# Attention with 16 x 8 heads on one core: steps of the fourth kind make four pairs of tiles in a row and the value product in one piece

## Chip, cores and metric

The kernel runs on one core of one Trainium2 chip. The metric is device time in microseconds (us); less is better. One execution was taken with the hardware profiler on; its rows are read below. TensorE is PE in the rows (its weight loads are PEld), VectorE is DVE, ScalarE is ACT, GpSimd is POOL and SyncE is SP.

## The reference, cut to what matters

```python
# x: [16 images, 128 channels, 32*32 pixels], fp32
hid = group_norm(x, 32 groups)
q, k, v = qkv_w @ hid + qkv_b            # 8 heads of 16 channels, 1024 pixels
weight = softmax((q * s).T @ (k * s))    # per image and head: 1024 x 1024
h = proj_w @ (v @ weight.T) + proj_b
x = x + h
# then, per image
x = x + conv_w @ gelu(rmsnorm(x)) + conv_b
x = x + ffn_w2 @ gelu(ffn_w1 @ rmsnorm(x) + ffn_b1) + ffn_b2
```

The change touches the attention alone: for each image and head a 1024 x 1024 table of scores, its maximum over the keys, its exponential, and the product with the values.

## The kernel before

**Units and steps.** A unit is one image with four of its heads; there are 32 units, two to an image (half 0 and half 1). A unit has 16 steps: two halves of 512 query pixels times eight chunks of 128 key pixels. In one step TensorE makes three sorts of products.

- Four score tiles S0 to S3 (`scores`, L714), one for each head: 128 keys by 512 queries, contraction over 64 rows. They go to PSUM banks 0, 1 and 2 in turn (`tile % BANKS`, `BANKS = 3`). ScalarE takes the exponential of each (L985) into `probs`. A score tile waits on `probs_ready` until the exponential of the tile three before it is done (L713), since that frees its bank.
- Four maximum tiles M0 to M3 (`maximum_scores`, L699): the same scores the other way round, 128 queries by 512 keys, made 13 steps ahead (`LEAD`), so that the maximum of each query is known before its scores are made. VectorE reduces each (L1093). They go round a ring of four PSUM banks (`RING_BANKS = (3, 4, 5, 7)`), and each waits on `max_taken` or another signal until whatever held the place four before it has been read (`wait_for_place`, L683).
- The value product V (`weigh_values`, L730): four matmuls, one for each head, each on 32 of the 128 columns of the array, which add the previous step's exponentials times the values to bank 6. Each is recorded as two, so a V of 512 columns has eight records. V waits for the last exponential of the previous step.

An S and an M use different halves of the array's rows when they stand side by side, and the trace shows them starting within 0.01 us of each other. The text calls these two a pair.

**Side jobs.** Small products that belong to other images (projections of queries, keys and values, the group statistics, the output projection) are put in the middle of a step (`side_jobs`, L628). A side job takes a place in the ring of four banks too, between M1 and M2 of its step (the loop at L306 counts it at `k == 2`). Steps of the fourth kind have a side job at two places only: step 3 and step 7 of half 0 of the images 0 to 13 (`GROUP_MEAN`, L639, and `GROUP_VAR`, L647), each a matmul of one column. Every step of the second kind has a side job in most of the kernel: not in the first unit and the first step of the second, and only in some steps of the last three.

**Order.** No scheduler is at work: each engine's instructions stand as they are written, and TensorE takes them in that order. There are four kinds of step, `s % 4` from 0 to 3:

```text
first  (s % 4 == 0):  S0 M0 M1 S1 S2 M2  job  V  S3 M3
second (s % 4 == 1):  M0 S0 S1 M1  job  M2 S2 S3 M3  V
third  (s % 4 == 2):  M0 S0 S1 M1 M2 S2  job  V  S3 M3
fourth (s % 4 == 3):  S0 M0 M1 S1  job  V[0:256]  M2 S2 S3 M3  V[256:512]
```

ScalarE takes the four exponentials of a step in the order of their tiles, and the copy of the finished sums (L927) and the side jobs' results stand between them. VectorE takes the four maxima of a step, and at some steps a few small operations (L1072, L1079, L1109, L1120). After the last unit a second part follows (L890 on): the rest of the block for all images.

The last unit makes maximum tiles no more from its step 3 on, since they run 13 steps ahead: there a step has only S and V.

Of the kernel before, what the change touches and what calls it, by code (L numbers as in the profile page):

```python
# [33 lines left out]
HALF = 512  # L34
# [14 lines left out]
HB = HIDDEN // 128  # L49
CONV, FIRST = 2, 4  # L50
EARLY_X = 3
QUARTER = 256


LAST_K, GROUP_MEAN, VALUES, GROUP_VAR, PROJ = (0, 1), (0, 3), ((0, 5), (0, 9)), (0, 7), ((0, 13), (1, 1))
# [58 lines left out]
def has_unit(u):  # L114
    return not is_number(u) or 0 <= u < UNITS
# [12 lines left out]
def build(nc, d):  # L128
    fp32, fp32r = mybir.dt.float32, mybir.dt.float32r
    ALU, ACT, AX = mybir.AluOpType, mybir.ActivationFunctionType, mybir.AxisListType  # L130
    with ExitStack() as ctx:
# [71 lines left out]
        def steps_of(part):  # L203

            return {None: range(STEPS), 0: range(5), 1: range(5, 7), 2: range(7, 10), 3: range(10, STEPS)}[part]
# [402 lines left out]
        def _(pe):  # L608
# [80 lines left out]
            def maximum_scores(u, s, k):  # L689
                unit, step = max_item(u, s)  # L690
                place = unit % RING
                if not has_unit(unit):
                    return
                j, key_half, p, chunk, tile = k % 2, k // 2, step % 2, step // 2, max_tile(u, s, k)
                used = slice(ROWS * j, ROWS * j + MAX_ROW)
                if step == 0 and k == 0:
                    pe.wait_ge(stack_in, unit * (16 * STACK_DMAS) + 16 * STACK_DMAS)
                wait_for_place(max_place[tile])
                nc.tensor.matmul(bank_of(max_place[tile]),  # L699
                                 q_stack[used, place, p, chunk % 4, chunk // 4, :],  # L700
                                 k_stack[used, place, p, HALF * key_half:HALF * key_half + HALF],
                                 start=True, stop=True).then_inc(max_ready, 1)

            def scores(u, place, s, k):

                if not has_unit(u):
                    return
                head, t, chunk, tile = score_head(k), s // NK, s % NK, u * TILES + 4 * s + k
                used = slice(ROWS * (head % 2), ROWS * (head % 2) + ROWS)
                p = head // 2  # L710
                if chunk == 0 and k == 0:
                    pe.wait_ge(rows_in, (NT * u + t + 1) * (16 * ROW_DMAS))
                at_least(pe, probs_ready, tile - BANKS + 1)  # L713
                nc.tensor.matmul(psum[:, tile % BANKS, :], k_stack[used, place, p, 128 * chunk:128 * chunk + 128],  # L714
                                 q_stack[used, place, p, :, t, :],
                                 start=True, stop=True).then_inc(scores_ready, 1)

            def weigh_values(u, parity, half, s, lo, hi):


                chunk = s % NK
                if lo == 0:
                    pe.wait_ge(probs_ready, u * TILES + (4 * s + 4))
                    if chunk == 0:
                        at_least(pe, acc_taken, u * NT + s // NK)
                    if s == 0 and half == 0:
                        pe.wait_ge(v_full, u + 2)
                for k in range(UNIT_HEADS):
                    g = score_head(k)
                    last = nc.tensor.matmul(acc[32 * g:32 * g + 32, lo:hi],  # L730
                                            values[:, parity, chunk, UNIT_HEADS * half + g, :],
                                            probs[:, (4 * s + k) % 8, lo:hi],
                                            start=(chunk == 0 and lo == 0), stop=(chunk == NK - 1),
                                            skip_group_check=True)
                if hi == HALF:
                    last.then_inc(pv_done, 1)

            def weigh_before(u, parity, half, s, lo, hi):

                if s == 0:  # L740
                    if has_unit(u - 1):
                        if half == 0:
                            weigh_values(u - 1, 1 - parity, 1, STEPS - 1, lo, hi)
                        else:
                            weigh_values(u - 1, parity, 0, STEPS - 1, lo, hi)
                elif has_unit(u):
                    weigh_values(u, parity, half, s - 1, lo, hi)

            def slot(b, parity, half, part=None):
                u = b * 2 + half  # L750
                for s in steps_of(part):
                    place = 2 * parity + half
                    if b == IMAGES - 1 and (half, s) == FIRST_CONV:
                        for k in range(3):
                            scores(u, place, s, k)
                        weigh_before(u, parity, half, s, 0, HALF)
                        pe.wait_ge(max_taken, UNITS * TILES)
                        pe.wait_ge(proj_taken, (IMAGES - 1) * NT)
                        pe.wait_ge(weights_split, 1)
                        convolve(0, 0)  # L760
                        convolve(0, 1)
                        scores(u, place, s, 3)
                        continue

                    if s % 4 == 0:
                        scores(u, place, s, 0)
                        maximum_scores(u, s, 0)
                        maximum_scores(u, s, 1)
                        scores(u, place, s, 1)
                        scores(u, place, s, 2)  # L770
                        maximum_scores(u, s, 2)
                        side_jobs(b, parity, half, s)
                        weigh_before(u, parity, half, s, 0, HALF)
                        scores(u, place, s, 3)
                        maximum_scores(u, s, 3)
                    if s % 4 == 1:
                        maximum_scores(u, s, 0)
                        scores(u, place, s, 0)
                        scores(u, place, s, 1)
                        maximum_scores(u, s, 1)  # L780
                        side_jobs(b, parity, half, s)
                        maximum_scores(u, s, 2)
                        scores(u, place, s, 2)
                        scores(u, place, s, 3)
                        maximum_scores(u, s, 3)
                        weigh_before(u, parity, half, s, 0, HALF)
                    if s % 4 == 2:
                        maximum_scores(u, s, 0)
                        scores(u, place, s, 0)
                        scores(u, place, s, 1)  # L790
                        maximum_scores(u, s, 1)
                        maximum_scores(u, s, 2)
                        scores(u, place, s, 2)
                        side_jobs(b, parity, half, s)
                        weigh_before(u, parity, half, s, 0, HALF)
                        scores(u, place, s, 3)
                        maximum_scores(u, s, 3)
                    if s % 4 == 3:
                        scores(u, place, s, 0)
                        maximum_scores(u, s, 0)  # L800
                        maximum_scores(u, s, 1)
                        scores(u, place, s, 1)
                        side_jobs(b, parity, half, s)
                        weigh_before(u, parity, half, s, 0, QUARTER)
                        maximum_scores(u, s, 2)
                        scores(u, place, s, 2)
                        scores(u, place, s, 3)
                        maximum_scores(u, s, 3)
                        weigh_before(u, parity, half, s, QUARTER, HALF)

            def product(out, weights, high, low):

# [5 lines left out]
            def convolve(c, t):  # L818

                if t == 0:  # L820
                    pe.wait_ge(act1_split, c + 1)
                at_least(pe, conv_taken, c * NT + (t - 1))
                half = slice(HALF * t, HALF * t + HALF)
                high, low = (act1_second_high, act1_second_low) if c == 1 else (act1_high, act1_low)
                product(psum[:, CONV_BANKS[t], :], (wconv_high[:, :], wconv_low[:, :]),
                        high[:, half], low[:, half]).then_inc(conv_ready, 1)
# [86 lines left out]
            nc.tensor.matmul(misc[:, 0:1], wp[:, :], params[:, V_B:V_B + 1], start=True, stop=True).then_inc(bias_ready, 1)  # L913
            pe.wait_ge(bias_taken, 1)
            run(pe, slot, lead_in, refine, project_last)


# [407 lines left out]
```

## Time and profile before

| | us |
|---|---|
| median of three runs | 1671.47 |
| lowest and highest | 1670.27, 1671.72 |
| the profiled execution, its own time | 1672.58 |
| its span, first to last instruction | 1670.6 |

| engine | busy us | share of the span |
|---|---|---|
| PE | 1606.7 | 96% |
| DVE | 1454.5 | 87% |
| ACT | 1341.3 | 80% |
| POOL | 335.6 | 20% |

The attention fills the span from 76.1 us (the first V) to 1419.7 us (the last V). A step takes some 2.6 us of it, four steps some 10.4 to 10.5 us. A timeline row gives the start, the duration and the engine; rows with "xN" merge N instructions that follow each other, and the duration then reaches from the first one's start to the last one's end. Durations of matmuls include the filling and draining of the array, so that the pace is read from one start to the next.

### The profile page before, as it was taken

How to read it: one execution, taken by the hardware profiler on the slowest of the kernel's cores; microseconds unless marked ns; L12 is line 12 of the kernel's file. 1: busy time of each engine (PE TensorE's matmuls, PEld its weight loads, DVE VectorE, ACT ScalarE, POOL GpSimd, SP SyncE). 2: the span in 40 equal slices, each digit the busy share in tenths (PEclk: the TensorE clock that was granted, in tenths of full speed). 3: DMA queues.
4: the chain of work that ended last, by engine and by line, in shares of the span. 5: the costliest groups of instructions: out<-in, count | busy, mean ns of one | idle time of the engine just before them, and what ended most of it. 6: DMA issues, size and time to landing. Idle time of an engine off the chain costs nothing.

```text
span 1670.6 us, 29685 instructions
## 1 busy us (share of the span) xinstructions
PE 1606.7 (96%) x10602; PEld 673.0 (40%) x10602; DVE 1454.5 (87%) x2415; ACT 1341.3 (80%) x2478; POOL 335.6 (20%) x411
## 2 busy tenths in 40 slices
PE   4999999999999999999999999999999998899999
PEld 2433333333333333333333333333333332455555
DVE  4999999999999999999999999999999994455552
ACT  2288888888888888888888888888888887666664
POOL 3101111111111111111121212121211122322220
PEclk9599999999999999999999999999999998999999
DMA  5233333333333333333333333333333320234332
GB/s 115 32 47 59 59 59 60 59 60 59 58 61 58 60 58 61 58 61 58 61 58 60 58 61 58 49 56 50 56 50 57 50 60 29 84 115 115 88 105 75
DMA packets 58610, 105.91 MB, mean 63 GB/s; under 512 B 32864, under 2 KB 33632, under 8 KB 58464
## 3 DMA queue, kind: packets, MB, share of 16 engines
q1 hardware_dynamic: 56160, 95.64, 33.8%
q10 hardware_dynamic: 2304, 8.39, 1.2%
q8 instruction: 84, 1.38, 0.4%
q14 instruction: 62, 0.51, 0.1%
HBM read 34.48 MB, written 9.05 MB: 26 GB/s over the span
## 4 chain that ended last, share of the span: by engine, by line
PE 89%; ACT 4%; DVE 3%; SPq 1%; issue 1%; DMA 1%; POOL 0%; DVEq 0%; ACTq 0%; POOLq 0%
PE psum L730 31%; PE psum L714 19%; PE psum L699 15%; PE psum L843 7%; PE psum L625 4%; ACT probs L985 4%; PE psum L814 2%; PE psum L816 2%; PE psum L815 2%; PE psum L617 2%; DVE maxes L1093 2%; PE psum L662 2%; PE psum L851 1%; SPq L357 1%; DMA q_stack<-rows 0%
## 5 line engine op out<-in xcount | busy, mean ns | idle before, releaser
L1093 DVE TENSOR_REDUCE maxes<-psum 128x1 f32<-128x512 f32 x2048 | 1270.7, 681 | 54.3 <-PE psum L699 45.9
L985 ACT ACTIVATE probs<-psum 128x512 f32<-128x512 f32 x2048 | 1093.2, 601 | 199.3 <-PE psum L714 180.3
L699 PE MATMUL psum<-k_stack,q_stack 62*128 62x512 f32 x2048 | 697.9, 442 | 1.7 <-DVE maxes L1093 0.9
L714 PE MATMUL psum<-q_stack,k_stack 64*128 64x512 f32 x2048 | 691.8, 439 | 5.3 <-ACT probs L985 4.2
L730 PE MATMUL psum<-probs,values 128*32 128x512 f32 (+1 forms) x5120 | 573.7, 520 | 22.0 <-ACT probs L985 22.0
L714 PEld LDWEIGHTS psum<-q_stack,k_stack 64*128 64x128 f32 x2048 | 326.8, 186 | 322.8 <-ACT probs L985 278.3
L699 PEld LDWEIGHTS psum<-k_stack,q_stack 62*128 62x128 f32 x2048 | 333.3, 188 | 250.9 <-DVE maxes L1093 188.2
L730 PEld LDWEIGHTS psum<-probs,values 128*32 128x32 f32 x5120 | 100.8, 108 | 225.1 <-issue 140.2
L479 POOL CAST parts<-neg_max 128x16 fp32r<-128x16 f32 x64 | 12.6, 197 | 554.9 <-DVE neg_max L1072 554.9
L843 PE MATMUL psum<-probs,first_weights 128*128 128x512 f32 x256 | 116.6, 598 | 0.9 <-DVE raw L1261 0.9
L995 ACT ACTIVATE probs<-psum,params_sb 128x512 f32<-128x512 f32 x128 | 82.3, 686 | 21.3 <-PE psum L816 14.9
L625 PE MATMUL psum<-hid,first_weights 128*128 128x512 f32 x128 | 75.8, 686 | 6.2 <-POOL hid L511 6.2
L528 POOL TENSOR_TENSOR x_sb<-attn,x_sb 128x512 f32<-128x512 f32 x32 | 41.2, 1290 | 177.9 <-ACT attn L970 177.5
L843 PEld LDWEIGHTS psum<-probs,first_weights 128*128 128x128 f32 x256 | 47.3, 189 | 60.8 <-issue 52.9
L814 PE MATMUL psum<-q_stack,q_high 128*128 128x512 f32 x128 | 57.5, 449 | 0.7 <-DVE q_stack L1194 0.7
L1200 DVE COPY sums<-psum 128x512 f32<-128x512 f32 x16 | 11.1, 692 | 52.0 <-PE psum L851 52.0
L1194 DVE TENSOR_TENSOR q_stack<-q_full,q_stack 128x1024 fp32r<-128x1024 f32 x16 | 19.6, 1226 | 36.8 <-ACT q_stack L1051 36.8
L1261 DVE SCALAR_TENSOR_TENSOR raw<-psum,params_sb,x_sb 128x512 f32<-128x512 f32 x32 | 24.0, 750 | 31.6 <-PE psum L843 31.6
L1030 ACT ACTIVATE hid<-x_sb 128x1024 f32<-128x1024 f32 x14 | 14.9, 1062 | 45.1 <-DVE x_sb L1164 45.1
L549 POOL TENSOR_TENSOR rms_out<-mean_eps,neg_halves 128x16 f32<-128x16 f32 x17 | 50.4, 2963 | 1.3
L816 PE MATMUL psum<-q_stack,q_low 128*128 128x512 f32 x128 | 50.4, 394 | 0.0
L815 PE MATMUL psum<-q_stack,q_high 128*128 128x512 f32 x128 | 50.3, 393 | 0.0
(95 smaller groups left out, 931.1 us busy)
## 6 DMA issues: line engine op xcount, KB each, us to landing
q_stack<-q_high SPq DMA_DIRECT2D x128, 128.0 KB, 4.0
k_stack<-k_high SPq DMA_DIRECT2D x128, 128.0 KB, 5.2
values<-inv_rms_rows SPq DMA_DIRECT2D x32, 512.0 KB, 5.1
x_sb<-in_x SPq DMA_DIRECT2D x16, 512.0 KB, 7.6
q_stack<-q_low SPq DMA_DIRECT2D x64, 128.0 KB, 6.3
k_stack<-k_low SPq DMA_DIRECT2D x64, 128.0 KB, 7.0
q_stack<-rows SPq DMA_DIRECT2D x512, 2.0 KB
attn<-raw SPq DMA_DIRECT2D x128, 64.0 KB, 2.3
```

Of the source, the lines that this page charges most:

```text
L549: nc.gpsimd.tensor_tensor(out=rms_out[:, :], in0=mean_eps[:, :], in1=neg_halves[:, :], op=ALU.pow).then_inc(rms_ready, 1)
L625: nc.tensor.matmul(qk_bank(c, n), weight[:, :], hid[:, HALF * t:HALF * t + HALF], start=True, stop=True).then_inc(qk_ready, 1)
L699: nc.tensor.matmul(bank_of(max_place[tile]), q_stack[used, place, p, chunk % 4, chunk // 4, :], k_stack[used, place, p, HALF * key_half:HA ...
L714: nc.tensor.matmul(psum[:, tile % BANKS, :], k_stack[used, place, p, 128 * chunk:128 * chunk + 128], q_stack[used, place, p, :, t, :], sta ...
L730: last = nc.tensor.matmul(acc[32 * g:32 * g + 32, lo:hi], values[:, parity, chunk, UNIT_HEADS * half + g, :], probs[:, (4 * s + k) % 8, lo ...
L814: nc.tensor.matmul(out, w_high, high, start=True, stop=False)
L815: nc.tensor.matmul(out, w_high, low, start=False, stop=False)
L816: return nc.tensor.matmul(out, w_low, high, start=False, stop=True)
L843: mm = nc.tensor.matmul(psum[:, OUT_BANK, :], w2[:, at:at + 128], act2(t, m), start=(m == 0), stop=(m == HB - 1))
L985: nc.scalar.activation(probs[:, tile % 8, :], psum[:, tile % BANKS, :], ACT.Exp, scale=SCALE).then_inc(probs_ready, 1)
L995: nc.scalar.activation(act2(t, m), psum[:, HIDDEN_BANKS[m], :], ACT.Gelu, bias=params[:, FFN_B1 + m:FFN_B1 + m + 1]).then_inc(act2_ready, 1)
L1093: nc.vector.tensor_reduce(maxes[:, chunk // 4, j, 4 * p + chunk % 4, key_half:key_half + 1], bank_of(max_place[max_tile(u, s, k)]), axis=A ...
```

## The change

In steps of the fourth kind the value product is no longer made in two pieces of 256 columns, one after S1 and one after M3. It is made in one piece of 512 columns behind M3, so that M2, S2, S3 and M3 follow directly on M0, S0, S1, M1 (and the side job, where there is one). The order is then that of the second kind, but for S0 and M0. Nothing else is changed; no other engine's instructions move.

```diff
 EARLY_X = 3
-QUARTER = 256
...
                         maximum_scores(u, s, 1)
                         scores(u, place, s, 1)
                         side_jobs(b, parity, half, s)
-                        weigh_before(u, parity, half, s, 0, QUARTER)
                         maximum_scores(u, s, 2)
                         scores(u, place, s, 2)
                         scores(u, place, s, 3)
                         maximum_scores(u, s, 3)
-                        weigh_before(u, parity, half, s, QUARTER, HALF)
+                        weigh_before(u, parity, half, s, 0, HALF)
```

Because `QUARTER` is gone, line numbers after it are one lower (L714 becomes L713, L730 becomes L729).

The order on PE shows it. First, a step of the fourth kind without a side job, from the last pair of the third kind to the first score tile of the next step, before:

```order
L714 MATMUL psum<-q_stack,k_stack 128x512 [waits probs_ready]
L699 MATMUL psum<-k_stack,q_stack 128x512 [waits max_taken]
L714 MATMUL psum<-q_stack,k_stack 128x512 [waits probs_ready]
L699 MATMUL psum<-k_stack,q_stack 128x512 [waits max_taken] x2
L714 MATMUL psum<-q_stack,k_stack 128x512 [waits probs_ready]
L730 MATMUL psum<-probs,values 32x256 [waits probs_ready]
L730 MATMUL psum<-probs,values 32x256 x3
L699 MATMUL psum<-k_stack,q_stack 128x512 [waits max_taken]
L714 MATMUL psum<-q_stack,k_stack 128x512 [waits probs_ready] x2
L699 MATMUL psum<-k_stack,q_stack 128x512 [waits max_taken]
L730 MATMUL psum<-probs,values 32x256 x4
L714 MATMUL psum<-q_stack,k_stack 128x512 [waits probs_ready]
```

The same place on PE in the changed kernel (L713 is S, L698 is M, L729 is V):

```order
L713 MATMUL psum<-q_stack,k_stack 128x512 [waits probs_ready]
L698 MATMUL psum<-k_stack,q_stack 128x512 [waits max_taken]
L713 MATMUL psum<-q_stack,k_stack 128x512 [waits probs_ready]
L698 MATMUL psum<-k_stack,q_stack 128x512 [waits max_taken] x2
L713 MATMUL psum<-q_stack,k_stack 128x512 [waits probs_ready]
L698 MATMUL psum<-k_stack,q_stack 128x512 [waits max_taken]
L713 MATMUL psum<-q_stack,k_stack 128x512 [waits probs_ready] x2
L698 MATMUL psum<-k_stack,q_stack 128x512 [waits max_taken]
L729 MATMUL psum<-probs,values 32x512 [waits probs_ready]
L729 MATMUL psum<-probs,values 32x512 x3
L713 MATMUL psum<-q_stack,k_stack 128x512 [waits probs_ready]
```

Eight matmuls of 256 columns have become four of 512, and five pairs now stand between one V and the next, where three and two stood. Second, on PE, step 7 of half 0 of an image, from M0 on, with its side job L647, before:

```order
L699 MATMUL psum<-k_stack,q_stack 128x512 [waits max_taken] x2
L714 MATMUL psum<-q_stack,k_stack 128x512 [waits probs_ready]
L647 MATMUL psum<-gn,first_weights 128x1 [waits max_taken,gn_mix]
L730 MATMUL psum<-probs,values 32x256 [waits probs_ready]
L730 MATMUL psum<-probs,values 32x256 x3
L699 MATMUL psum<-k_stack,q_stack 128x512 [waits max_taken]
L714 MATMUL psum<-q_stack,k_stack 128x512 [waits probs_ready] x2
L699 MATMUL psum<-k_stack,q_stack 128x512 [waits max_taken]
L730 MATMUL psum<-probs,values 32x256 x4
```

The same place on PE in the changed kernel, where the job's line is L646:

```order
L698 MATMUL psum<-k_stack,q_stack 128x512 [waits max_taken] x2
L713 MATMUL psum<-q_stack,k_stack 128x512 [waits probs_ready]
L646 MATMUL psum<-gn,first_weights 128x1 [waits max_taken,gn_mix]
L698 MATMUL psum<-k_stack,q_stack 128x512 [waits max_taken]
L713 MATMUL psum<-q_stack,k_stack 128x512 [waits probs_ready] x2
L698 MATMUL psum<-k_stack,q_stack 128x512 [waits max_taken]
L729 MATMUL psum<-probs,values 32x512 [waits probs_ready]
L729 MATMUL psum<-probs,values 32x512 x3
```

With a side job the two last maximum tiles now follow the job directly, with no V between them; the signals they wait for are the same as before.

## Rows read from the trace of the kernel before

**Rows 1.** The page, parts 1 and 2: busy us, and tenths in 40 slices.

```profile
PE 1606.7 (96%) x10602; PEld 673.0 (40%) x10602; DVE 1454.5 (87%) x2415; ACT 1341.3 (80%) x2478; POOL 335.6 (20%) x411
PE   4999999999999999999999999999999998899999
PEclk9599999999999999999999999999999998999999
```

**Rows 2.** Waits of PE over the span: us in total, times, longest us.

```profile
PE psum L730 <- ACT probs L985: 22.0, 100, 0.6
PE psum L714 <- ACT probs L985: 4.2, 9, 0.5
```

**Rows 3.** Timeline of PE, fourth kind, no job: start us, us, engine, line.

```profile
706.23 0.49 PE L714 MATMUL psum<-q_stack,k_stack 64*128 64x512 f32 x1
706.56 0.63 PE L714 MATMUL psum<-q_stack,k_stack 64*128 64x512 f32 x2
706.80 0.40 PE L699 MATMUL psum<-k_stack,q_stack 62*128 62x512 f32 x1
707.41 0.64 PE L730 MATMUL psum<-probs,values 128*32 128x256 f32 x8 [0.20 <-ACT probs L985]
707.98 0.50 PE L699 MATMUL psum<-k_stack,q_stack 62*128 62x512 f32 x1
...
708.64 0.64 PE L730 MATMUL psum<-probs,values 128*32 128x256 f32 x8
709.21 0.49 PE L714 MATMUL psum<-q_stack,k_stack 64*128 64x512 f32 x1
```

**Rows 4.** Timeline of ACT at the same place, from 706.5 to 707.7 us.

```profile
706.76 1.08 ACT L985 ACTIVATE probs<-psum 128x512 f32<-128x512 f32 x2 [0.38 <-PE psum L714]
```

**Rows 5.** Timeline of PE, second kind without a job, in unit 29.

```profile
1317.45 0.50 PE L714 MATMUL psum<-q_stack,k_stack 64*128 64x512 f32 x1
...
1318.64 0.99 PE L714 MATMUL psum<-q_stack,k_stack 64*128 64x512 f32 x2
1319.13 0.49 PE L699 MATMUL psum<-k_stack,q_stack 62*128 62x512 f32 x1
1319.56 1.07 PE L730 MATMUL psum<-probs,values 128*32 128x512 f32 x8
1320.56 0.50 PE L699 MATMUL psum<-k_stack,q_stack 62*128 62x512 f32 x1
```

**Rows 6.** Timeline of ACT there, from 1317.9 to 1318.9 us.

```profile
1317.99 1.09 ACT L985 ACTIVATE probs<-psum 128x512 f32<-128x512 f32 x2 [0.33 <-PE psum L714]
```

**Rows 7.** Timeline of PE, fourth kind with job L639, in unit 10.

```profile
496.73 0.50 PE L714 MATMUL psum<-q_stack,k_stack 64*128 64x512 f32 x1
...
497.63 0.38 PE L639 MATMUL psum<-mean_var,first_weights 128*128 128x1 f32 x2
497.94 0.64 PE L730 MATMUL psum<-probs,values 128*32 128x256 f32 x8
...
499.75 0.50 PE L714 MATMUL psum<-q_stack,k_stack 64*128 64x512 f32 x1
```

**Rows 8.** Timeline of DVE there: from 497.3 to 497.9 us, and to 498.5.

```profile
497.30 0.69 DVE L1093 TENSOR_REDUCE maxes<-psum 128x1 f32<-128x512 f32 x1 [0.17 <-PE psum L699]
497.30 1.29 DVE L1093 TENSOR_REDUCE maxes<-psum 128x1 f32<-128x512 f32 x2 [0.17 <-PE psum L699]
```

**Rows 9.** Timelines of DVE and PEld in the first maxima, one after the other.

```profile
48.51 0.68 DVE L1093 TENSOR_REDUCE maxes<-psum 128x1 f32<-128x512 f32 x1
49.23 0.28 PEld L699 LDWEIGHTS psum<-k_stack,q_stack 62*128 62x128 f32 x1 [0.32 <-DVE maxes L1093]
```

**Rows 10.** Timeline of PE in the last unit, without M: fourth kind, then second.

```profile
1374.54 0.50 PE L714 MATMUL psum<-q_stack,k_stack 64*128 64x512 f32 x1
1377.29 1.17 PE L714 MATMUL psum<-q_stack,k_stack 64*128 64x512 f32 x3
...
1411.07 0.73 PE L714 MATMUL psum<-q_stack,k_stack 64*128 64x512 f32 x3
1414.16 0.49 PE L714 MATMUL psum<-q_stack,k_stack 64*128 64x512 f32 x2
```

## The prediction, made before the changed kernel ran

> **What bounds the kernel now.** I read the page first. TensorE is busy for 96% of the span and at full tenths in nearly every slice of the attention, so what lengthens its line lengthens the kernel; VectorE comes next with 87%. The granted clock is at its upper level in nearly all slices [rows 1]. Then the waits of PE: it stood idle before V for 22.0 us, 100 times, always for an exponential, and before score tiles for 4.2 us in all [rows 2]. The 100 are steps of the fourth kind. There are 128 of these (four in each of 32 units); 28 have a side job (step 3 and step 7 of half 0, images 0 to 13), which fills the gap, and 100 have none: 96 in units 0 to 30 and all four of unit 31.
>
> Then the timeline of one such step, counted from S3 of the third kind at 706.23, the first tile behind a V. Two more pairs start at 706.56 and 706.80. The first piece of V starts only at 707.41, having waited 0.20 for the exponential of that S3; M2 and S2 follow 0.57 later at 707.98, the second piece at 708.64, and S0 of the next step at 709.21 [rows 3]. That is 2.98 us from V's end to V's end. No other wait of this size stands on PE between this step and the next fourth one, so a step of the fourth kind that grows by x makes the kernel grow by x.
>
> **What is removed.** Four matmuls a step, and one turn from tiles to V and back. From rows: a piece of 256 columns takes 0.57, the two 1.14, and one V of 512 columns 1.00 (1319.56 to 1320.56) [rows 3, 5]: 0.14 less. In the middle of a run, a pair follows a pair after 0.24 (706.56 to 706.80), but the first after V takes 0.33 and so does the last before V [rows 3]: runs of three and two pairs (0.90 + 0.66) become one run of five (0.33 + 3 x 0.24 + 0.33 = 1.38), 0.18 less. And the 0.20 of idle time ahead of V goes. That is 0.5 us a step, if PE could run freely.
>
> The Trainium skill has a rule for the second of these, on the page "TensorEngine Tiling (Array Packing)", Key Properties: changing the tiling mode, rather than just the tile, drains the engine. The trace agrees, with the 0.33 against 0.24. By the rule alone the change saves time; it is the mechanism of the second rival below.
>
> **What it runs into.** Score tiles have three banks. S2 waits for the exponential of the third kind's S3, and S3 for that of the S0 in its own step. Between them stood a piece of V, which took up just this time. Now PE reaches them early. The two exponentials end at 706.76 + 1.08 = 707.84 for the second [rows 4]; a waiting tile starts about 0.05 after (1317.99 + 1.09 = 1319.08, tile at 1319.13) [rows 5, 6]. So S3 and M3 start at 707.89 and not 708.32. V starts 0.43 behind a pair that had waited (1319.13 to 1319.56) and takes 1.00 [rows 5]: next S0 at 709.32, against 709.21. The step is 0.11 longer.
>
> The trace has this very order already, in steps of the second kind that have no side job. There five pairs stand in a row, and PE goes from S3 at 1317.45 to the first tile behind V at 1320.56 [rows 5]: 3.11 us against 2.98, 0.13 longer. ScalarE's times there are the same from the first tile on (0.54, then 1.09 for two exponentials, against 0.53 and 1.08) [rows 4, 6]. So the parts give 0.11 and the analogue 0.13, each with a rounding of 0.01; I take 0.115, nearer the parts, which are of this very step. **96 steps x 0.115 = 11.0 us.**
>
> The maximum tiles in these steps wait for nothing later: M3 takes the place of the third kind's M3, whose reduction ends 1.26 after the first tile (496.73 to 497.99) [rows 7, 8], while S3 starts at 1.66.
>
> **The 28 steps with a side job** are another matter. The job takes one of the four places of the ring, between M1 and M2. So M2 takes that of the third kind's M3, and M3 that of M0 in its own step. Before, V stood between and nobody waited. M0's reduction ends at 497.30 + 1.29 = 498.59 [rows 8]; a weight load that waits for VectorE starts 0.04 to 0.05 after it (48.51 + 0.68 = 49.19, then 49.23) [rows 9]. M3 therefore starts at 498.64, 0.24 later than S3 could. M2 is held as well, to 497.99 + 0.05 = 498.04, but S3 may not start before 498.40 anyway. V at 498.64 + 0.43 = 499.07, next S0 at 500.07, against 499.75 now [rows 7]: 0.32 longer. **28 x 0.32 = 9.0 us.** This is the least sure term, as no row shows M3 held so. If M0's reduction came in time the step would be 3.10 long against 3.02: 0.08, or 2.2 us for 28. I take 0.32, since VectorE reduces without a pause from M3 of the third kind on (1.29 for two, 0.60 each) and cannot come sooner.
>
> **The last unit** has no M from step 3 on. Its fourth step goes from 1374.54 to 1377.29, 2.75 us; a second-kind step with the new order, from 1411.07 to 1414.16, 3.09 [rows 10]. 0.34 longer, times four: **1.4 us**, between 0 (one of them hides behind the next part's first loads) and 1.8.
>
> **The sum:** 11.0 + 9.0 + 1.4 = 21.4 us. The profiled execution took 1672.58, which makes 1694.0; the median of three runs lies 1.1 lower: 1692.9.
>
> Nothing hides this. What is queued behind the waiting S3 on PE is M3, V and the whole next step. ScalarE gets S2 and S3 earlier than now, but it already idles before the next step's S0, so that buys nothing; VectorE needs 16 x 0.60 = 9.6 us of four steps' 10.4 [rows 8] and is not the end.
>
> **Rivals.**
>
> 1. *Slower, but by less:* M3 isn't held in the 28 steps. 11.0 + 2.2 + 1.4 = 14.6 us, 1686.1. Against it: the ring has four places, and the job takes one. 13%.
> 2. *Faster:* tiles flow at PE's pace. A fourth step would be 1.38 + 1.00 = 2.38 long: 0.60 less in 96 steps and 0.64 less in 28, together 75 us, so 1596; VectorE's 9.6 us for four steps wouldn't forbid it. This is what the rule on draining would give if nothing else bound. The point where it decides is the start of S3: 0.43 + 1.00 = 1.43 us stand behind it, so the step gets shorter only if S3 starts by 2.98 - 1.43 = 1.55 after the first tile. The rows put it at 1.66, since S0's bank is read only then. For the rival speaks only that the waits on PE now are short ones [rows 2]. 5%.
> 3. *No change:* a later wait gets shorter by as much as this one grows. All waits of V together were 22.0 us and go with the pieces; 4.2 us of the others is all that could give [rows 2], so 1692.9 would become 1688.7 at best, and it is within 0.2% only if M3's hold fell away and the analogue misled too. 2%.
> 4. *Much slower:* M3 is held in every fourth step, as in the 28: to 3.34 against 2.98, 0.36 x 96 = 34.6, with 9.0 and 1.4 45 us: 1716.5. It needs a reduction that ends 0.4 later than the rows say. 5%.
>
> The forecast has the remaining 75%.
>
> **How the numbers follow.** The predicted time is the forecast's, 1692.9. The low end takes in rival 1 without a good part of the last unit's term (1686.1 - 1.4 = 1684.7, rounded to 1684); the high end has 0.13 for 0.115 (1.4 us more), 1.8 for 1.4 in the last unit, and 0.37 for 0.32 in the 28 (1.4 us more): 1696.1, rounded to 1697. Beyond lie rivals 2, 3 and 4 with 12% between them. A measurement of this kernel can tell about 0.2%, 3.3 us, from no change. Slower by more: forecast, rivals 1 and 4, 93%. Within: 2%. Faster: 5%.
>
> **What would show it.** In the changed kernel's timeline, a fourth step without a job should look like the second kind's in unit 29: S2 about 1.18 and S3 about 1.66 after the first tile, V at 2.10, next tile at 3.10. With a job, M3 alone at 1.91, V at 2.34, next tile at 3.34. The waits of PE should name ScalarE at score tiles instead of V, and VectorE at M3 in 28 steps; four steps take 10.5 to 10.6 us for 10.4. PEclk should stay where it is, since the new idle times are 0.25 us long and the first unit, whose second-kind steps have such waits already, shows the upper level. The prediction is wrong if V starts within 1.98 us after the first tile, or if the steps with and without a job grow alike.

## The result: 13.6 us slower

| | median of runs, us | lowest and highest | profiled span, us |
|---|---|---|---|
| before | 1671.60 | 1670.27, 1672.01 | 1670.6 |
| changed | 1685.18 | 1684.14, 1685.42 | 1683.4 |

The ratio is 1.0081, its 95% interval 1.0064 to 1.0099, so the kernel is slower, as forecast, and by 13.6 us where the forecast had 21.4: the time lies inside the range, near its low end, at the time of the first rival (1686.1), though not for its reason. Some runs below had an execution in a slower state of the chip (one each of e3, e7 and c2): ratios and their intervals leave it out, the medians of those three would be 0.09 to 0.14 us lower without it, and the trace of e7_red_before is of such an execution and isn't read.

The page of the changed kernel, parts 1 and 2, answers to [rows 1]:

```profile
PE 1640.5 (97%) x9578; PEld 683.9 (41%) x9578; DVE 1465.3 (87%) x2415; ACT 1327.6 (79%) x2478; POOL 336.0 (20%) x411
PE   4999999999999999999999999999999998899999
PEclk9699999999999999999999999999999999999999
```

PE has 1024 records less and is *busy* 33.8 us more. That is the first thing to read here: busy time on PE is not work. A matmul's record lasts some 0.5 us while the next may start after 0.24 [rows 3], so PE can stand held for 0.2 us with no idle time on the page. The waits of the changed kernel show it (engine, line, what it waited for: us in total, times, longest), and answer to [rows 2]; the last row is of the weight loads:

```profile
PE psum L713 <- ACT probs L983: 4.7, 13, 0.5
PE psum L698 <- DVE maxes L1091: 0.9, 2, 0.5
...
PEld psum L713 <- ACT probs L983: 361.5, 582, 0.9
```

The 22.0 us ahead of V are gone, and PE's own waits for score tiles have hardly grown (4.2 to 4.7). It is the *weight loads* that tell of the new waits: those of score tiles waited 361.5 us for exponentials, where the kernel before has:

```profile
PEld psum L714 <- ACT probs L985: 278.3, 477, 0.9
```

A step of the fourth kind without a job, PE's timeline in the changed kernel, answers to [rows 3]:

```profile
522.77 0.50 PE L713 MATMUL psum<-q_stack,k_stack 64*128 64x512 f32 x1
522.78 0.73 PE L698 MATMUL psum<-k_stack,q_stack 62*128 62x512 f32 x2
523.11 0.62 PE L713 MATMUL psum<-q_stack,k_stack 64*128 64x512 f32 x2
523.35 0.61 PE L698 MATMUL psum<-k_stack,q_stack 62*128 62x512 f32 x2
523.96 0.99 PE L713 MATMUL psum<-q_stack,k_stack 64*128 64x512 f32 x2
524.45 0.50 PE L698 MATMUL psum<-k_stack,q_stack 62*128 62x512 f32 x1
524.88 1.06 PE L729 MATMUL psum<-probs,values 128*32 128x512 f32 x8
525.87 0.50 PE L713 MATMUL psum<-q_stack,k_stack 64*128 64x512 f32 x1
```

From the first tile S2 comes at 1.19, S3 (with M3) at 1.68, V at 2.11, the next step at 3.10. It was 2.98. And one with the job, in unit 10, step 3, the place of [rows 7]:

```profile
501.24 0.49 PE L713 MATMUL psum<-q_stack,k_stack 64*128 64x512 f32 x1
...
502.15 0.38 PE L638 MATMUL psum<-mean_var,first_weights 128*128 128x1 f32 x2
502.55 0.50 PE L698 MATMUL psum<-k_stack,q_stack 62*128 62x512 f32 x1
502.55 0.85 PE L713 MATMUL psum<-q_stack,k_stack 64*128 64x512 f32 x2
503.15 0.50 PE L698 MATMUL psum<-k_stack,q_stack 62*128 62x512 f32 x1
503.57 1.06 PE L729 MATMUL psum<-probs,values 128*32 128x512 f32 x8
504.57 0.50 PE L713 MATMUL psum<-q_stack,k_stack 64*128 64x512 f32 x1
```

M2 starts at 1.31, M3 alone at 1.91, V at 2.33, the next step at 3.33. VectorE's timeline there, the answer to [rows 8]:

```profile
501.80 1.29 DVE L1091 TENSOR_REDUCE maxes<-psum 128x1 f32<-128x512 f32 x2 [0.15 <-PE psum L698]
```

The second of these is the reduction of M0; it ends at 503.09, and M3 starts 0.06 later.

So both kinds of step have the shape that was forecast, to within 0.02 us. Where are the missing 8 us? From the start of each step's S0 to the next, in both traces, summed by sort of step (changed kernel less the kernel before; both traces are of one execution, so that their spans differ by 12.8 us and the medians by 13.6):

| | steps | forecast, us | measured, us |
|---|---|---|---|
| fourth kind without a job, units 0 to 30 | 96 | +11.0 | +10.2 |
| fourth kind with a job | 28 | +9.0 | +8.6 |
| all other steps of units 0 to 30 | 372 | 0 | -3.3 |
| last unit | 16 | +1.4 | -2.1 |
| before the first S0 | | 0 | -0.6 |
| after the last score tile | | 0 | -0.1 |
| span | | +21.4 | +12.8 |

### The profile page after: what moved, and what is told of

Read it like the earlier page. It is cut to its first block, busy times and chain, and to the rows that moved or that the text cites. A ratio compares the mean times of both kernels' runs of the same rounds, so it can differ in the third digit from the quotient of the medians.

```text
span 1683.4 us, 27637 instructions
## 1 busy us (share of the span) xinstructions
PE 1640.5 (97%) x9578; PEld 683.9 (41%) x9578; DVE 1465.3 (87%) x2415; ACT 1327.6 (79%) x2478; POOL 336.0 (20%) x411
## 4 chain that ended last, share of the span: by engine, by line
PE 95%; DVE 2%; ACT 1%; SPq 1%; issue 1%; POOL 0%; DMA 0%; ACTq 0%; DVEq 0%; POOLq 0%
PE psum L729 30%; PE psum L713 25%; PE psum L698 16%; PE psum L841 7%; PE psum L624 4%; PE psum L812 2%; PE psum L813 2%; PE psum L814 2%; PE psum L616 2%; PE psum L661 2%; DVE maxes L1091 1%; PE psum L849 1%; ACT probs L983 0%; PE psum L638 0%; PE psum L646 0%
## 5 line engine op out<-in xcount | busy, mean ns | idle before, releaser
L713 PE MATMUL psum<-q_stack,k_stack 64*128 64x512 f32 x2048 | 717.1, 443 | 5.4 <-ACT probs L983 4.7
L698 PE MATMUL psum<-k_stack,q_stack 62*128 62x512 f32 x2048 | 701.8, 442 | 2.6 <-DVE maxes L1091 0.9
L729 PE MATMUL psum<-probs,values 128*32 128x512 f32 x4096 | 545.5, 605 | 0.0
L713 PEld LDWEIGHTS psum<-q_stack,k_stack 64*128 64x128 f32 x2048 | 336.0, 185 | 435.3 <-ACT probs L983 361.5
L698 PEld LDWEIGHTS psum<-k_stack,q_stack 62*128 62x128 f32 x2048 | 341.9, 188 | 209.0 <-DVE maxes L1091 187.5
L729 PEld LDWEIGHTS psum<-probs,values 128*32 128x32 f32 x4096 | 80.6, 108 | 157.6 <-issue 110.3
```

What stands on the lines that cost most here:

```text
L698: nc.tensor.matmul(bank_of(max_place[tile]), q_stack[used, place, p, chunk % 4, chunk // 4, :], k_stack[used, place, p, HALF * key_half:HA ...
L729: last = nc.tensor.matmul(acc[32 * g:32 * g + 32, lo:hi], values[:, parity, chunk, UNIT_HEADS * half + g, :], probs[:, (4 * s + k) % 8, lo ...
```

## The experiments

All are compared with the kernel before, run beside them (medians 1671.92, 1671.02 and 1671.70 in the three groups).

### The parts of the change alone

The edit for the first three is the same with three conditions in place of `C`:

```diff
                         side_jobs(b, parity, half, s)
-                        weigh_before(u, parity, half, s, 0, QUARTER)
+                        whole = C
+                        if not whole:
+                            weigh_before(u, parity, half, s, 0, QUARTER)
                         ...
-                        weigh_before(u, parity, half, s, QUARTER, HALF)
+                        weigh_before(u, parity, half, s, 0 if whole else QUARTER, HALF)
```

**e1_job_steps**, `C`: half 0, steps 3 and 7, images 0 to 13.

> The change in the 28 fourth-kind steps with a side job alone; the other 100 as before. Theory A (M3 is held until M0 of its own step is reduced, because the job has taken a place in the ring): each of the 28 grows by 0.31 us as in the profile of the changed kernel (8.6 us in all), less a small give-back in other steps of some 0.7: about 8 us over before, 1679.5. Rival B (these steps grow no more than the others, 0.08 to 0.11 each, and the profile misleads): 2 to 3 us, 1674.

Measured: 1677.62 us, ratio 1.0038 (1.0025 to 1.0050), 5.7 us over before. In its trace the 28 steps take 9.3 us more, the 96 others the same to 0.1, all other steps 0.4 less. The first S0 came 2.7 us earlier in that execution, though nothing ahead of it had changed; whether it did so in the others too, which would explain most of the gap between 9 and the median, isn't known. The step's growth is theory A's; rival B's 2 to 3 us is below the interval (4.2 us at least).

**e2_no_job_steps**, `C`: not those, and not the last unit.

> The change in the 96 fourth-kind steps without a job of units 0 to 30 alone. Theory A (S3 waits for the exponential of S0): 0.107 us each as the changed kernel's profile has it, 10.2 us, less a give-back of 2 to 3 us that the other steps showed in that profile: 7.5 to 8 us, 1679. Rival B (the give-back belongs to the steps with a job alone): the full 10.2 us, 1681.8.

Measured: 1679.29 us, ratio 1.0047 (1.0034 to 1.0059), 7.4 us over before. In its trace the 96 steps take 10.6 us more and the 372 others 3.0 us less. So nearly all of the give-back comes with the steps without a job.

**e3_last_unit**, `C`: `u == UNITS - 1`.

> The change in the four fourth-kind steps of the last unit alone. My prediction had 1.4 us for these. Theory A, from the changed kernel's profile: a fourth step there grows by 0.34 but the first-kind step after it shrinks by 0.42, since ScalarE sets the pace of both, so that the sum is within 0.3 us of nothing, 1671.5. Rival B: the unit got 2.1 us faster in that profile by the change, not by the clock's luck; then 1669.5. Rival C, as predicted: 1673.

Measured: 1671.65 us, ratio 1.0001 (0.9991 to 1.0010). Nothing, as theory A has it. In its trace the last unit is 0.1 us shorter, not 2.1. The medians of the three parts add up: 5.7 + 7.4 - 0.3 = 12.8 of 13.6. Each of them is uncertain by some 2 us, so that this is a rough check only.

### Does a cut cost anything by itself?

**e4_two_pieces**, the changed kernel with the two pieces of V side by side:

```diff
                         maximum_scores(u, s, 3)
-                        weigh_before(u, parity, half, s, 0, HALF)
+                        weigh_before(u, parity, half, s, 0, HALF // 2)
+                        weigh_before(u, parity, half, s, HALF // 2, HALF)
```

> The changed order, but V of the fourth kind in two pieces of 256 columns one behind the other, with no tiles between them: the cost of cutting alone. Theory A (each piece has a cost of its own, 1.14 for two against 1.00 for one): 0.14 us in 128 steps, 17.9 us over the changed kernel, 1703. Rival B (the cost of a piece is that of the turn between tiles and V, so that a piece behind a piece costs nothing): 1685.

Measured: 1686.24 us, ratio to before 1.0089 (1.0075 to 1.0103), 1.1 us over the changed kernel's median, which is within the noise, and 17 us under theory A. So rival B holds. PE's timeline at the end of such a step:

```profile
526.02 1.07 PE L729 MATMUL psum<-probs,values 128*32 128x256 f32 x16
527.02 0.50 PE L713 MATMUL psum<-q_stack,k_stack 64*128 64x512 f32 x1
```

Two pieces of 256 columns side by side take 1.00 us, as one of 512 does. So the 0.14 that I read as the cost of a cut is part of the turn: 1.00 us for V is 0.86 of columns and 0.14 of going over to the tiles.

### Who holds the tiles?

Six kernels leave work out. In the first pair each exponential covers 256 of 512 columns (`probs` is filled with ones beforehand), in the second pair each reduction of a maximum tile does. A third pair, further down, has both.

```diff
-    nc.scalar.activation(probs[:, tile % 8, :], psum[:, tile % BANKS, :],
+    nc.scalar.activation(probs[:, tile % 8, 0:HALF // 2], psum[:, tile % BANKS, 0:HALF // 2],
```

```diff
-    bank_of(max_place[max_tile(u, s, k)]),
+    bank_of(max_place[max_tile(u, s, k)])[:, 0:HALF // 2],
```

**e5_exp_before** and **e6_exp_after**, short exponentials:

> The kernel before, with each exponential over 256 of the 512 columns alone (the other half of the exponentials is left out and keeps a constant). Theory A (PE waits for exponentials): the 0.2 us ahead of V in 96 steps goes, 15 to 20 us under before, some 1653, unless VectorE, with 9.6 us and its small operations of four steps' 10.4, sets the end sooner: then some 1660. Rival B (exponentials do not matter): 1671.

> The changed kernel with each exponential over 256 columns alone (the other half left out). Theory A (S2 and S3 wait for exponentials and this alone makes the steps without a job longer): S3 comes by 1.2 us and these steps fall to about 2.6 us, 0.2 under the before with short exponentials; the 28 with a job stay at 3.34, since they wait for VectorE. Together some 10 us faster than the kernel before with short exponentials, or equal if VectorE bounds both. Rival B (something else of the order costs the 0.11): it stays 13 us slower than it.

Measured: 1642.29 us (ratio to before 0.9829, 0.9813 to 0.9845) and 1652.56 us (0.9889, 0.9874 to 0.9903). The kernel before fell by 28.7 us, more than the 15 to 20 expected: in its trace the 96 steps give 17.3 of it, the other steps of units 0 to 30 give 6.9, most of it in the third kind, and the rest lies in the last unit and behind it. The changed one is still 10.3 us slower, where I had expected it 10 faster or equal: the sign is wrong, and by the totals alone rival B (13 slower) would be the nearer. The traces decide it. From the first trace to the second, the 96 steps without a job now take 4.7 us *less* (with full exponentials 10.2 more), the 28 with a job 9.2 more, the other steps 2.4 more. (The sum is under 10.3, since the profiled execution of e5 was 3.3 us over its median.) PE in a step without a job, changed kernel with short exponentials:

```profile
515.03 0.50 PE L713 MATMUL psum<-q_stack,k_stack 64*128 64x512 f32 x1
...
516.01 0.77 PE L713 MATMUL psum<-q_stack,k_stack 64*128 64x512 f32 x2
516.36 0.50 PE L698 MATMUL psum<-k_stack,q_stack 62*128 62x512 f32 x1
516.78 1.06 PE L729 MATMUL psum<-probs,values 128*32 128x512 f32 x8
517.78 0.50 PE L713 MATMUL psum<-q_stack,k_stack 64*128 64x512 f32 x1
```

The step is 2.75 long instead of 3.10, so it was the exponentials that made it long. But the kernel before gains too, since its V waits for the same exponential (2.78 instead of 2.98), and M3 at 1.33 has found its next holder. VectorE's timeline there shows the reduction of the third kind's M3, which ends at 516.30, 0.06 ahead of M3:

```profile
515.61 0.69 DVE L1091 TENSOR_REDUCE maxes<-psum 128x1 f32<-128x512 f32 x1
```

I had counted the gain of the changed kernel and forgotten that of the kernel before.

**e7_red_before** and **e8_red_after**, short reductions:

> The kernel before, with each reduction of a maximum tile over 256 of 512 columns alone (the other half of the keys is left out of the maximum). VectorE is then far from the end. Theory A: some 3 us under before (the small give-back of other steps that the changed kernel showed is that PE now and then waits for VectorE): 1668. Rival B (the give-back is not VectorE's): 1671.

> The changed kernel with each reduction over 256 columns alone (the other half left out). Theory A (M3 is held by VectorE in the 28 steps): M3 comes with S3, these steps fall from 3.34 to 3.10, 6.5 us in all, and the difference to the kernel before with short reductions is 96 x 0.11 + 28 x 0.08 = 12.8 us; the kernel comes to some 1678 to 1680. Rival B (VectorE holds nothing): 1685, unchanged.

Measured: 1660.18 us (0.9931, 0.9915 to 0.9948) and 1670.53 us (0.9998, 0.9988 to 1.0007). The difference is 10.4 us, where I had 12.8. Both kernels are some 8 us faster than I expected (1668, and 1678 to 1680). Most of the fall against the kernels with full reductions lies ahead of the first S0, which comes 11.8 us earlier in the second one's trace than in the kernel before: the maxima that run ahead are made there at VectorE's pace [rows 9]. The job step, in the changed kernel with short reductions:

```profile
488.87 0.50 PE L713 MATMUL psum<-q_stack,k_stack 64*128 64x512 f32 x1
...
490.54 0.50 PE L698 MATMUL psum<-k_stack,q_stack 62*128 62x512 f32 x1
490.97 1.06 PE L729 MATMUL psum<-probs,values 128*32 128x512 f32 x8
491.96 0.50 PE L713 MATMUL psum<-q_stack,k_stack 64*128 64x512 f32 x1
```

M3 comes at 1.67, with S3, and the step is 3.09 long, not 3.33. The 28 take 2.6 us more than in the kernel before, 0.09 each, where they took 8.6; the 96 take 10.4 more, as with full reductions. So with full exponentials VectorE holds M3 in the job steps and nothing in the others.

**e9_both_before** and **e10_both_after**, both short:

> The kernel before with both short: exponentials and reductions over 256 columns each, the other halves left out. PE then runs at its own pace in the attention. Theory A: the 0.2 us ahead of V goes in 96 steps, 1650.

> The changed kernel with both short (other halves left out). Theory A (the change does save PE time, 0.14 for the cut and 0.18 for the turn, but waits ate it): 0.32 us in 124 steps less than the kernel before with both short, less what is still waited for by S3 (an exponential of half length ends at about 1.2 us, where PE's pace would have S3 at 1.06): 0.15 to 0.3 each, 20 to 38 us under it. Rival B (the change saves nothing on PE, so that the rule on turns has no size here): equal or slower.

Measured: 1623.84 us (0.9720, 0.9707 to 0.9733) and 1613.85 us (0.9657, 0.9643 to 0.9672). The first is 26 us under the 1650 expected, which had counted the wait ahead of V alone: in its trace the 96 steps take 19.3 us less than in the kernel before, but the other steps of units 0 to 30 take 12.7 less too, and the first S0 comes 8.1 earlier. With both engines faster the change *is* a gain, 10.0 us. It is less than the 20 to 38 expected. From the first trace to the second the 96 steps take 10.6 us less, the 28 take 3.5 less and the other steps 1.9 more. PE in a step without a job, first the changed kernel, then the one before, both short:

```profile
493.95 0.50 PE L713 MATMUL psum<-q_stack,k_stack 64*128 64x512 f32 x1
...
494.92 0.77 PE L713 MATMUL psum<-q_stack,k_stack 64*128 64x512 f32 x2
495.26 0.43 PE L698 MATMUL psum<-k_stack,q_stack 62*128 62x512 f32 x1
495.62 1.07 PE L729 MATMUL psum<-probs,values 128*32 128x512 f32 x8
496.62 0.49 PE L713 MATMUL psum<-q_stack,k_stack 64*128 64x512 f32 x1
```

```profile
498.42 0.49 PE L714 MATMUL psum<-q_stack,k_stack 64*128 64x512 f32 x1
...
499.39 0.64 PE L730 MATMUL psum<-probs,values 128*32 128x256 f32 x8
499.96 0.50 PE L699 MATMUL psum<-k_stack,q_stack 62*128 62x512 f32 x1
...
500.63 0.64 PE L730 MATMUL psum<-probs,values 128*32 128x256 f32 x8
501.20 0.50 PE L714 MATMUL psum<-q_stack,k_stack 64*128 64x512 f32 x1
```

2.67 against 2.78. Even half an exponential holds S2 to 0.97 and S3 to about 1.24, where PE's pace would have them at 0.81 and 1.05; that is why 0.11 us are saved in a step and not 0.3. (The kernel before still stands too, but only for 0.07 ahead of V, which comes at 0.97 and not at 0.90.)

### A version that the hole points to

In the kernel before PE stands for 0.28 us in 96 steps, between the end of the third pair and V. A part of the third kind's V may be put into the hole, ahead of the fourth kind's first piece (the expectations still counted 0.14 for a cut):

```diff
                     if s % 4 == 2:
...
-                        weigh_before(u, parity, half, s, 0, HALF)
+                        weigh_before(u, parity, half, s, 0, HALF - held_back(b, half, s + 1))
...
                     if s % 4 == 3:
...
+                        if held_back(b, half, s):
+                            weigh_before(u, parity, half, s - 1, HALF - held_back(b, half, s), HALF)
                         weigh_before(u, parity, half, s, 0, QUARTER)
```

`held_back` is 256 or 160 columns, and 0 where a job fills the hole.

> Not the change but what its failure points to: before, with V of the third kind cut to 256 columns and the other 256 made in the 0.28 us hole of the next fourth-kind step, ahead of its own first piece (96 steps and the four of the last unit; not where a job fills the hole). Theory A: a piece costs 0.14 + 0.43 for 512/2 columns in two passes, less the overlap; behind a V piece it takes 0.57 at the most. V of the third kind gets 0.43 shorter; the fourth step gets 0.57 - 0.28 = 0.29 longer: 0.14 us less in 96 steps, 13 us under before, 1658. Rival B (the piece holds back the exponential of S0, whose place in probs it reads, and with it S3 and the next step): no gain, 1671 or more.

> The same with 160 columns held back instead of 256. Theory A: V of the third kind 0.27 shorter, a piece of 160 columns 0.14 + 0.27 = 0.41 in a hole of 0.28: again 0.14 less in 96 steps, 1658, with less delay for the exponential. If the exponential is held back at 256 columns, this one is the faster of the two. Rival B: no gain, 1671.

Measured: **c1_held_back_256** 1682.57 us (1.0066, 1.0054 to 1.0079), **c2_held_back_160** 1667.74 us (0.9978, 0.9969 to 0.9988). The larger piece loses 10.9 us, the smaller gains 4.0, and neither gives the 13 expected. ScalarE's timelines, the larger first, name the cause:

```profile
521.36 2.07 ACT L990 ACTIVATE probs<-psum 128x512 f32<-128x512 f32 x4 [0.76 <-PE psum L730]
```

```profile
516.45 2.06 ACT L990 ACTIVATE probs<-psum 128x512 f32<-128x512 f32 x4 [0.46 <-PE psum L730]
```

These four begin with the exponential of S0. It writes to the place in `probs` that the piece held back still reads, so it starts 1.92 us after the step's first tile with 256 columns (519.44) and 1.59 with 160 (514.86), while in the kernel before it has ended by 1.61 [rows 3, 4]. S3 waits for it in turn: with 256 columns its pair starts at 522.01, 0.05 after that exponential ends. That is rival B for 256 columns, and a part of it for 160. Still, c2 is the fastest of all kernels here that compute everything, 0.22% under before.

## Why the prediction was right, and where it was off

**The bound, and that a grown step passes through.** Right for the fourth kind: the 124 steps alone are 18.8 us longer, of 20.0 forecast.

**Steps without a job, 0.115 each.** Measured 0.107 (10.24 / 96). The first tile to V was to be 2.10 and is 2.11. The analogue, steps of the second kind that have no job, was the right row to read. e6 shows the cause: with short exponentials the same steps shrink, from 3.10 to 2.75.

**Steps with a job, 0.32 each.** Measured 0.31. I called this the least sure term; M3 was to come at 1.91 and did. e8 takes VectorE's share away and leaves 0.09, where rival 1 had 0.08. So rival 1, which named the time, is refuted as a mechanism.

**The last unit, 1.4.** Mis-sized: nothing. The fourth steps do grow (0.34, 0.43 and 0.34 in the trace), but I looked at them alone. From its step 3 on the unit has no maximum tiles, and its runs of score tiles are paced by ScalarE, so the first-kind step behind each gets shorter (0.43, 0.25, 0.42). e3 puts the sum at zero. The -2.1 of the changed kernel's trace isn't that of the edit in this unit: it lies in step 6, where the first convolutions of the second part are made. The granted clock over the 26 us around it was 0.80 before and 0.93 in the changed kernel, and 0.80 in e3 with the same edit in this unit:

```profile
1372.00:1398.00 26.00, 21.80 (x120) 8.59 (x112) 17.82 (x23) 19.65 (x32) 6.39 (x5) 0.80 0.08 12
```

```profile
1386.00:1412.00 26.00, 21.54 (x111) 8.38 (x111) 19.85 (x24) 21.11 (x34) 6.50 (x6) 0.93 0.08 12
```

(The first is before, the second the changed kernel; the clock is the third number from the end.) e4's trace has 0.93 and 2.1 us less in this unit too, so chance isn't shown. But the whole time doesn't follow the clock: the four executions of the changed kernel had mean granted clocks of 0.985, 0.986, 0.983 and 0.983 and took 1685.40, 1684.95, 1684.14 and 1685.42 us. Why the clock fell for longer in one than in the other was not tried.

**"Nothing elsewhere gives back."** This is the step that failed, and its price is 3.3 us: the other 372 steps are 0.009 shorter each. The third rival had capped a give-back at the 4.2 us of [rows 2], but those 4.2 are still there (4.7), so what shrank isn't in that table. e2 has the give-back too (3.0), e1 hardly (0.4), so it comes with the steps without a job. Whether VectorE has a part in it, as I supposed before e8, is not settled. With short reductions the kernels differ by 10.4 us where 12.8 would be left if it went, but that difference is uncertain by some 3 us. In e8's trace the other steps take 2.0 less, but only against the kernel before with *full* reductions. With short exponentials it turns round (2.4 and 1.9 more in the others, e5 to e6 and e9 to e10). That points to ScalarE, which in the changed kernel has S2 and S3 earlier and is the sooner ready for what follows.

One such wait can be seen, in the weight loads of S2 in the steps of the first kind; it is a load for the bank of the fourth kind's S3. Here it is in the step behind [rows 3], and below it in the changed kernel, behind the step shown above:

```profile
709.68 0.18 PEld L714 LDWEIGHTS psum<-q_stack,k_stack 64*128 64x128 f32 x1 [0.17 <-ACT probs L985]
526.21 0.19 PEld L713 LDWEIGHTS psum<-q_stack,k_stack 64*128 64x128 f32 x1
```

Before, the load is held to 0.47 after the step's first tile; in the changed kernel it comes at 0.34 and waits for nothing. Of the 123 such steps behind a fourth one, 121 have the load held before and none in the changed kernel, and their mean length falls from 2.247 to 2.234. That is 1.5 of the 3.3 us. But e5's trace has no load held either, and steps of 2.244, so the load alone is not shown to be the cause. Of the other 1.8 us, 1.4 lie in the second kind. The cause stays open.

**What was saved.** I had two savings, 0.14 for the cut and 0.18 for the turn. e4 makes this one saving, the turn's, 0.32 us there and back (0.14 + 0.18, worked out from the rows). The Trainium skill's rule, on the page "TensorEngine Tiling (Array Packing)", Key Properties, that a change of tiling mode drains the engine, agrees more fully than I said: a second piece in the same mode costs nothing that e4 can tell from noise, and the price lies at the change of mode. The second rival, which rests on it, failed by S3's start (1.68, where it needed 1.55), and e10 shows a part of the saving (0.11 of 0.32) coming through once the other engines are fast.

**The signs to look for.** The times of the tiles came out. The table of waits did not: I had expected PE's own rows to name ScalarE at score tiles, and only the weight loads' rows do.

## What to carry to other kernels

A piece of work in the middle of a run of products may cost a turn of the engine and still pay, if it stands where the next product would have had to wait for its bank: here a piece of V of 0.57 us stood where S2 had to wait to 1.19 and S3 to 1.68 after the first tile. Before two such pieces are merged, write down for each product behind them when its bank comes free, and count every ring by itself, for a small job that takes a place in a ring shortens it for the rest of its step. Look for a stretch of the trace that already has the new order; here a step of another kind gave the new length to within 0.01 us (3.11 against 3.10).

## What the runs showed of the hardware

- Going from pair tiles (64 of the array's rows each) to V (32 of its columns each) and back costs 0.32 us on PE, by the pace of the rows; cutting V in two without leaving the mode costs nothing that can be told from noise (1.1 us in 128 steps, e4).
- PE's busy time rose by 33.8 us while its work fell. Held matmuls hide behind the records of those in front; here the weight loads' waits show them (278.3 us for exponentials before, 361.5 in the changed kernel).
- A tile held by another engine starts 0.05 to 0.06 us after that engine's instruction ends, and V starts 0.42 to 0.43 behind a pair that had been held, not 0.33.
